# Self-attention inside a fused block: row maxima spread over the block boundary, key tiles in another order, first cross-attention maxima one block earlier

## What is computed

```python
q = jnp.einsum('bsd,hde->bhse', q_in, Wq)      # 16 heads of 16
k = jnp.einsum('btd,hde->bhte', k_in, Wk)
scores = jnp.einsum('bhse,bhte->bhst', q, k) * scale
if causal:
    scores = jnp.where(mask, scores, -jnp.inf)  # 1024 x 1024, lower triangle
p = jax.nn.softmax(scores, axis=-1)
o = jnp.einsum('bhst,bhte->bhse', p, v)
```

## Time and profile before

| what | value |
|---|---|
| median of 3 runs | 1350.21 us (1333.12 to 1362.43) |
| profiled execution, its own time | 1346.83 us |
| its span | 1345.1 us |
| PE busy over the span | 1179.0 us (88%) |
| DVE busy | 857.1 us (64%) |
| ACT busy | 561.0 us (42%) |
| POOL busy | 314.9 us (23%) |
| mean granted TensorE clock | 0.939 of full |
| self-attention, blocks 1 to 8 | 96.15 to 418.33 us |
| DMAs of a group's pack (L1105) | 12 of 128 KB, median 5.6 us from issue to landing |

### The profile page before, as it was taken

How to read it: one execution, slowest core, us unless ns; L and a number is a source line. 1 busy time by engine, 2 the same in 40 slices (tenths; PEclk the granted TensorE clock), 3 DMA queues, 4 the chain that set the end, 5 groups by cost and what they waited for, 6 DMA issues and landing times. The chain is left out here.

```text
span 1345.1 us, 19850 instructions
## 1 busy us (share of the span) xinstructions
PE 1179.0 (88%) x7060; PEld 835.7 (62%) x7060; DVE 857.1 (64%) x1830; ACT 561.0 (42%) x1209; POOL 314.9 (23%) x490
## 2 busy tenths in 40 slices
PE   8788888878887899899888876999989798899999
PEld 4343333333333337777566755999977677789998
DVE  5476766677664768566568787756544445855555
ACT  6215556555565555454235453010023332543332
POOL 5022122232122036453237552000010112500000
PEclk9889999999998869998979888999999889999999
DMA  7740373330434511000030000000030000000000
GB/s 211 192 99 2 55 62 49 49 48 2 83 64 71 105 41 41 0 0 1 0 125 1 2 1 1 1 0 1 1 126 0 1 0 1 1 1 17 16 17 16
DMA packets 38000, 50.69 MB, mean 38 GB/s; under 512 B 11130, under 2 KB 28816, under 8 KB 37264
## 3 DMA queue, kind: packets, MB, share of 16 engines
q1 hardware_dynamic: 37904, 49.44, 17.8%
HBM read 37.26 MB, written 11.77 MB: 36 GB/s over the span
## 5 line engine op out<-in xcount | busy, mean ns | idle before, releaser
L561 PE MATMUL PS<-ARENA 128*17 128x512 f32 (+17 forms) x2208 | 404.3, 425 | 79.7 <-DVE ARENA L1731 25.8
L561 PEld LDWEIGHTS PS<-ARENA 128*17 128x17 f32 (+6 forms) x2208 | 164.5, 126 | 251.9 <-issue 136.1
L1333 ACT ACTIVATE ARENA<-PS 128x512 f32<-128x512 f32 (+3 forms) x384 | 173.8, 493 | 145.1 <-PE PS L561 141.6
L1731 DVE TENSOR_REDUCE ARENA<-PS 128x1 f32<-128x128 f32 (+7 forms) x256 | 179.4, 749 | 70.6 <-PE PS L561 69.7
L561 PE MATMUL PS<-WQKVP,TRR 128*128 128x384 f32 x512 | 134.2, 344 | 1.5 <-ACT BC L1260 1.0
L2176 POOL TENSOR_SCALAR_AFFINE_SELECT ARENA<-ARENA 128x128 f32<-128x128 f32 x256 | 74.9, 302 | 204.3 <-ACT ARENA L1333 201.0
L2144 POOL TENSOR_TENSOR rstd<-var,halves 128x4 f32<-128x4 f32 x36 | 38.4, 1065 | 261.1 <-DVE var L1559 214.7
L561 PEld LDWEIGHTS PS<-W2P,INT 128*128 128x128 f32 x768 | 95.1, 188 | 2.9
L561 PE MATMUL PS<-W2P,INT 128*128 128x256 f32 x768 | 95.6, 280 | 0.0
L561 PEld LDWEIGHTS PS<-WQKVP,TRR 128*128 128x128 f32 x512 | 93.6, 192 | 2.6 <-ACT BC L1260 1.9
L561 PE MATMUL PS<-TRR,W1P 128*128 128x512 f32 x256 | 88.4, 406 | 7.1 <-ACT BC L1260 7.1
(11 more groups left out here) (223 smaller groups left out, 1966.8 us busy)
## 6 DMA issues: line engine op xcount, KB each, us to landing
ARENA<-qk_parts SPq DMA_DIRECT2D x96, 128.0 KB, 5.6
ARENA<-xq_parts SPq DMA_DIRECT2D x48, 128.0 KB, 5.9
qk_parts<-ARENA SPq DMA_DIRECT2D x6, 768.0 KB, 3.3
ARENA<-in_w SPq DMA_DIRECT2D x2, 2048.0 KB, 10.5
xq_parts<-ARENA SPq DMA_DIRECT2D x8, 384.0 KB, 2.3
ARENA<-in_wqkv SPq DMA_DIRECT2D x1, 3072.0 KB, 9.9
X<-in_x SPq DMA_DIRECT2D x4, 512.0 KB, 7.4
ARENA<-in_wf SPq DMA_DIRECT2D x2, 1024.0 KB, 8.2
```

The lines of the kernel that those rows point to most:

```text
L561: return nc.tensor.matmul(o, lhsT, rhs, start=start, stop=stop, **kw)
L1333: ins = nc.scalar.activation(PROB[GRP * (step % 2) + j][:, 0:w], PS[:, uses[key][0], 0:w], ACT.Exp, scale=HD ** -0.5)
L1731: ins = v.tensor_reduce(negm[:, n % 2, TPB * j + st:TPB * j + st + 1], PS[:, bank:bank + 2, :].rearrange("p b s -> p (b s)")[:, 0:P * (st ...
```

## The change

- The maxima of group m (m at least 1) are placed by a new function, `maxima_places`, over a window of 48 units that begins at unit 38 of block m - 1 and ends at unit 37 of block m, in proportion to the same work estimates. "neg" goes to unit 39 (`NEG_AT`); at that unit it stands ahead of maxima, elsewhere nothing changes in a unit's order. Group 0 stays as it was.
- The steps go, in widths: 512, 128, 384, 256 for c = 0, and 512, 128, 512, 256, 512, 384, 512, 512 for c = 1. Diagonal are the steps 0 to 3, 5, 7, 9 and 11. The start and stop flags of the PV sums, the count that PE waits for from POOL and the "last score" that SP waits for follow the new order.
- The xmax of chunk 0 go to units 40 to 47 of block 7, xneg of chunk 0 to unit 2 of block 8.
- POOL's `power` for the norms of blocks 5, 6 and 8 goes from piece 0 to piece 4 of the norm, since a diagonal step now lies between them.
- Later, ahead of the splitting of the feed-forward's hidden rows, POOL waits for the last drained "xo" bank.

```diff
-STEPS = [(tt, c) for c in range(2) for tt in range(4 * (c + 1))]
+STEPS = [(0, 0), (3, 0), (1, 0), (2, 0), (0, 1), (7, 1), (1, 1), (6, 1), (2, 1), (5, 1), (3, 1), (4, 1)]
+FIRST_OF = [next(tt for tt, half in STEPS if half == c) for c in range(2)]
+LAST_OF = [[tt for tt, half in STEPS if half == c][-1] for c in range(2)]
+DIAGONAL = [tt for tt, c in STEPS if c == tt // 4]
+LAST_SCORE = STEPS[-1] + (3,)
...
-LEAD, NEG_LEAD, PV_LAG, OUT_AT, STEP_WEIGHT, ROW_WEIGHT = 15, 10, 2, 6, 600, 1000
+NEG_AT, PV_LAG, OUT_AT, STEP_WEIGHT, ROW_WEIGHT = 39, 2, 6, 600, 1000
...
+def maxima_places():
+    places = {}
+    units = len(STEPS) * GRP
+    steps_work = [STEP_WEIGHT + 512 * (c + 1) - max(P * tt, 512 * c) for tt, c in STEPS for _ in range(GRP)]
+    for m in range(GROUPS):
+        maxima = [(j, st) for j in range(GRP) for st in ROW_ORDER]
...
+        window = [(m - 1, u) for u in range(NEG_AT - 1, units)] + [(m, u) for u in range(NEG_AT - 1)]
+        work = [ROW_WEIGHT + P * (st + 1) for _, st in maxima]
+        done, passed = 0, 0
+        total = sum(steps_work[u] for _, u in window)
+        for n, u in window:
+            passed += steps_work[u]
+            while done < len(maxima) and sum(work[:done + 1]) * total <= passed * sum(work):
+                places.setdefault((n, u), []).append(("max", m) + maxima[done])
+                done += 1
...
+                if u >= NEG_AT + 1:
+                    yield "xmax", 0, u % 4, u // 4 - (NEG_AT + 1) // 4
             if n == GROUPS:
-                if u < 8:
-                    yield "xmax", 0, u % 4, u // 4
-                if u == 9:
+                if u == 2:
                     yield "xneg", 0
...
+            elif u != NEG_AT:
+                yield from places.get((n, u), [])
+            if u == NEG_AT and n < GROUPS:
                 yield "neg", n
+                yield from places.get((n, u), [])
...
-                        pe.wait_ge(cleared, GRP * (TPB * n + tt + 1))
+                        pe.wait_ge(cleared, GRP * (TPB * n + DIAGONAL.index(tt) + 1))
...
-                    elif op == "norm" and at[0] == 0:
+                    elif op == "norm" and at[0] == 4:
                         power("g1", n)
...
                 if (name, k) == ("g3", 0):
+                    drained(pool, ("xo", XSTEPS - 1))
                     lower_units(0, range(FCH))
```

More of the change, by code:

```diff
@@ L97 @@
 G2_PIECES = 6
+def maxima_places():
[4 more added lines that the diff above has]
+        maxima = [(j, st) for j in range(GRP) for st in ROW_ORDER]
+        if m == 0:
+            for k, at in enumerate(maxima):
+                places.setdefault((0, k // 2), []).append(("max", 0) + at)
+            continue
+        window = [(m - 1, u) for u in range(NEG_AT - 1, units)] + [(m, u) for u in range(NEG_AT - 1)]
[7 more added lines that the diff above has]
+                done += 1
+        assert done == len(maxima)
+    return places
 def attention_plan():
+    places = maxima_places()
     for n in range(GROUPS + 1):
-        maxima = [(j, st) for j in range(GRP) for st in ROW_ORDER] if n < GROUPS else []
         units = len(STEPS) * GRP
-        steps_work = [STEP_WEIGHT + 512 * (c + 1) - max(P * tt, 512 * c) for tt, c in STEPS for _ in range(GRP)]
-        maxima_work = [ROW_WEIGHT + P * (st + 1) for _, st in maxima]
-        done = 0
         for u in range(units):
@@ L152, in attention_plan @@
                     yield "xqm", 2, u // 2 - 22
[L153 to L165, removed]
+            if n == 0 and u < PROJ_STEPS:
+                yield from places.get((n, u), [])
+                yield "project", n, u
+            elif u != NEG_AT:
+                yield from places.get((n, u), [])
+            if u == NEG_AT and n < GROUPS:
                 yield "neg", n
+                yield from places.get((n, u), [])
             if n > 0 and u % GRP == PV_LAG and u > GRP:
@@ L751, in _ @@
                     tt, c, j = at
-                    if (tt, c, j) == (0, 0, 0):
+                    if (tt, c, j) == STEPS[0] + (0,):
                         if n == 0:
@@ L766, in _ @@
                     tt, c = at
-                    if (tt, c) == (0, 0):
+                    if (tt, c) == (FIRST_OF[0], 0):
                         claim(("values", n, 0), [6], signals=0)
@@ L770, in _ @@
                             drained(pe, ("v1", i))
-                    if (tt, c) == (0, 1):
+                    if (tt, c) == (FIRST_OF[1], 1):
                         claim(("values", n, 1), [6], signals=0)
@@ L781, in _ @@
                                  VEXT[:, TPB * b + tt, GRP * (n % 4) + j, :],
-                                 PROB[GRP * (STEPS.index((tt, c)) % 2) + j][:, 0:w], start=tt == 0, stop=tt == 4 * c + 3)
+                                 PROB[GRP * (STEPS.index((tt, c)) % 2) + j][:, 0:w], start=tt == FIRST_OF[c], stop=tt == LAST_OF[c])
                     ins.then_inc(pv_done, 1)
@@ L1163, in _ @@
                     send_queries(0)
-                    arrived(sp, ("score", GROUPS - 3, TPB - 1, 1, GRP - 1))
+                    arrived(sp, ("score", GROUPS - 3) + LAST_SCORE)
                     load_queries(0)
@@ L1171, in _ @@
                 if 1 <= n < GROUPS - 2:
-                    arrived(sp, ("score", n - 1, TPB - 1, 1, GRP - 1))
+                    arrived(sp, ("score", n - 1) + LAST_SCORE)
                     load_pack(n + 2)
-            arrived(sp, ("score", GROUPS - 2, TPB - 1, 1, GRP - 1))
+            arrived(sp, ("score", GROUPS - 2) + LAST_SCORE)
             load_queries(1)
```

## The result

The changed kernel took 1329.1 us (median of 20 runs, 1322.9 to 1339.7), the kernel before 1344.9 beside it. The ratio is 0.990, 95% interval 0.988 to 0.993: 1% faster, where 1326 us and 1.5% were forecast. The profiled executions went from 1346.8 to 1335.9 us.

What follows compares the result with a forecast made beforehand. No engine was full: PE and DVE wait for each other mid-block, both for the exponential-clearing-PV chain at its end. Terms -18.3 - 0.5 - 4.8 - 0.5 + 3.5 = -20.6 from 1346.8 gave 1326 us; range 1303 to 1350.

Steps and rivals of the forecast that it cites:

- The plain block: Blocks 2 to 4, without norm or cross maxima: about 38 us before, forecast 33.5, range 31 to 38.6.
- two bounds: For the new plain block: DVE's work at 81.5% plus the border, 32.4 us; PE busy 33.2 plus 1.2 waiting, 34.4.
- the new order by itself is 0.9 us dearer: Plain block's floor without maxima: 29.0 us in the new step order against 28.1, because the last PV is wide.
- Maxima in front of the PV: Each maximum costs 0.30 us wherever it stands; block 38.6 us, total about 1354, slower than before; chance 0.13.
- The clock: PE's clock falls more often: two more such stretches in each of seven blocks, 12 us, total 1338; chance 0.08.
- Block 8: Eight xmax leave (-2.4), order adds 0.9 and power 1.2; forecast -0.5 us, range 0 to -4.
- the loads are costed at nothing: Packs are issued at a block's start, needed over 25 us later, and land in about 6; no cost.
- The power, priced at 1.2: POOL's power between heads of step 7 delays three clearings and that step's PV; 0 to 3 us, taken as 1.2.
- The start: Ahead of block 1, seven maxima delay the last two warming matmuls: +3.5 us, range 0 to 4.9.
- Block 1: Falls to the plain block's 33.5 us plus the 1.9 it keeps for the context's keys.
- Blocks 5 and 6: DVE's norm in steps 5 to 8 adds about 6 us, power 1.2; together 81.4 us against 81.9, -0.5.
- Block 7: 33 reductions in place of 32; keeps its 9.2 us surplus over a plain block: 42.7 us, -4.8.

Runs made afterwards that it cites:

- narrow_end: The changed kernel with the second half's diagonal steps reordered so each block ends on its narrowest step (128 wide, not 512); 1322.7 us, ratio to before 0.988.
- place_only: The changed kernel with the steps back in the old order, the maxima keeping their new window; 1330.6 us, ratio to before 0.992.
- order_only: The changed kernel with the new step order, but maxima of groups 1 to 7 kept within their own block; 1347.0 us, ratio to before 1.003.
- xmax_back: The changed kernel with the eight xmax of chunk 0 back in block 8; one profile: block 7 41.5 us, block 8 42.6 us.
- power_late: The changed kernel with POOL's power at norm piece 6 in blocks 5 and 6, piece 7 in block 8; one profile: block 8 42.7 us.

## Why the prediction came near, and where its steps failed

By terms, from the two profiles (the forecast's first, then the measured): start +3.5, +5.4; block 1 -4.7, -1.8; blocks 2 to 4 -13.5, -13.6; blocks 5 and 6 -0.5, -5.1; block 7 -4.8, -3.4; block 8 -0.5, +6.0; sum -20.6, -12.4. The medians moved by 15.8. The total is near because errors of both signs stand in it, and that is luck: the start (+5.4, given as 0 to 4.9) and block 8 (+6.0, given as 0 to -4) lie outside their own ranges.

- **The plain block** held in size: 33.5 forecast, 33.47 measured, DVE busy 75% in it and the border's ACT idle above 2.5 us, as said. That it hit so closely is luck too. It was the middle of two bounds, and the one by PE (34.4) did not hold: it took PE's busy 33.2 us as fixed work, which held step 0 at the lower clock, and PE is now busy 30.6. The one by DVE (32.4) was passed by narrow_end, 32.26. The reason held in part. Waits of the chain are now filled with maxima. But that the order of steps is what brings them there is refuted by place_only, and "the new order by itself is 0.9 us dearer" by order_only (2.3 cheaper). The floor prices steps without maxima and says nothing of how order and maxima meet. In block 3, 1.0 us of order_only's gain is the full clock of step 0 (2.54 in place of 3.57); how the order alone wins the rest is open. What the floor said of the last PV is shown by narrow_end.
- **Maxima in front of the PV** (the third rival) needed 0.30 us for each of 32; over the floor of 29.0 they cost 4.5 / 32 = 0.14 us. It is out. Its price had been read with step 0 at a granted 0.58 in it: without those 1.15 us, steps 0 to 3 give (4.3 - 1.15) / 14 = 0.22.
- **The clock** (second rival) went the other way in the plain blocks: 0.95 to 0.98 before, 1.00 now. Short waits in each diagonal step did not let it fall, and so the Trainium skill's rule of small idles between groups of matmuls (page "TensorE: Matmul & The Clock Gate", section "A second HAM failure mode: psum-queue depth-cycling") did not decide here: round the border of block 2 PE waits 0.81 and then 0.53 us, at a steady 1.00. In blocks 5 and 8 it did fall, from 0.97 to 0.91 and 0.85.
- **Block 8** is the failed step, in two terms. The first is "the loads are costed at nothing". It was worked out for the packs of keys, not for the second pack of queries, which is issued 2.5 us ahead of block 8 and used in steps 3 and 4. Without the eight xmax the first four steps take 8.7 us where they took 12.0 (9.0 in the old order), and PE comes to the second half of the pack before it has landed. Steps 4 to 7 then take 16.3 us where they take 11.6 with a later use: 4.8 us (2.5 where the pack landed earlier), which eats the 3.3 us won ahead of them. So taking the eight xmax out, priced at -2.4, wins nothing in block 8. The second term is the order, priced at 0.9: steps 8 to 11 take 4.1 us more than in place_only, 1.5 of them in the wide last step (5.20 against narrow_end's 3.69). Why steps 8 to 10 are longer is not shown. The power, priced at 1.2, costs nothing: steps 8 and 9 take 9.0 us with it at piece 0 and at piece 4 in the old order, 11.0 at piece 4 and 11.2 at piece 7 in the new. The forecast's own sentence, that the turn goes on waiting for the norm's last piece, was the right one.
- **The start** was mis-sized by 1.9 us: it took the seven maxima to be paced by DVE at 0.70 us each, but the stretch from "neg" to the warming matmuls ran at a granted 0.50 (the eight matmuls behind "neg" take 1.81 us where they took 1.03) and grew by 5.95 us, and the warming behind it gave back only 0.55. In place_only and narrow_end, whose orders of steps put five and six maxima there, that stretch ran at 0.62 and 0.67 and the start grew by 3.4 and 3.9. How much of the 1.9 is the clock is not shown.
- **Block 1** kept 4.9 us over a plain block (38.37 - 33.47), not 1.9. Its context work stands in steps 1 and 3 (3.86 and 4.77 us against 2.67 and 1.99 in block 3), which no longer have waits to hide it; step 10, with 14 DVE instructions in place of 7, adds 1.3. That is read from the trace alone; no run took the context work out.
- **Blocks 5 and 6.** The norm adds 5.3 and 4.5 us to a plain block, not 6 (3.7 and 4.5 at the full clock, by block 5 of xmax_back), and the power nothing that shows: from 262 to 320 us PE's longest waits are 1.48 us for DVE's maxima, once in each block, and its only waits for POOL are 0.81 at the borders. The wait for POOL in step 7 that the forecast named is not there; it stands in block 8 (3.00 us), where taking it away only lengthens the wait for the norm.
- **Block 7** lacks 1.4 us of its gain. The eight xmax cost it 2.7 (xmax_back), where their count had been set against the seven maxima that leave.

## What to carry to other kernels

Where two engines wait for each other in one part of a loop body and both wait for a chain in another, spread the filler over the whole body before changing the order of the chain: here the spreading alone gave the whole gain of the equal blocks. Whoever makes a stretch shorter should look up what is loaded behind it, with its issue time and first use, since a load that was just in time may now be late. Look for an edit's gain in the steps that it touches: power_late had the forecast 1.9 us in its block, but in steps where it changed nothing. A gain in equal blocks is easy to forecast; the first and last, which hold work that the others lack, decide how much of it is left.
